# Causal attention with a two-pass softmax on one core: the causal cut of the second pass moves from TensorE to GpSimd

## The reference

```python
scores = jnp.einsum('bhqd,bhkd->bhqk', Q, K) * scale
causal = jnp.triu(jnp.ones((s, s), dtype=bool), k=1)
scores = jnp.where(causal[None, None], -jnp.inf, scores)
attn = jax.nn.softmax(scores, axis=-1)
out = jnp.einsum('bhqk,bhkd->bhqd', attn, V)
```

## Time and profile before

| | |
|---|---|
| median of three runs | 1615.28 us (1613.65 to 1616.12) |
| profiled execution | 1615.37 us, span of its instructions 1613.6 us |
| TensorE (PE) busy | 1501.3 us, 93% |
| VectorE (DVE) busy | 811.3 us, 50% |
| ScalarE (ACT) busy | 545.0 us, 34% |
| GpSimd (POOL) busy | 216.3 us, 13%, nearly all behind 1015 us |
| mean granted TensorE clock | 0.958 of full speed |

### The profile page before, as it was taken

How to read it: one execution, slowest core, us unless ns; L and a number is a source line. 1 busy time by engine, 2 the same in 40 slices (tenths; PEclk the granted TensorE clock), 3 DMA queues, 4 the chain that set the end, 5 groups by cost and what they waited for, 6 DMA issues and landing times.

```text
span 1613.6 us, 22531 instructions
## 1 busy us (share of the span) xinstructions
PE 1501.3 (93%) x6818; PEld 788.3 (49%) x6819; DVE 811.3 (50%) x2073; ACT 545.0 (34%) x1130; POOL 216.3 (13%) x296
## 2 busy tenths in 40 slices
PE   3997999999999997899999966799999999999996
PEld 2553233343433332455555535566666666666663
DVE  2898988888788840666666649211111111111111
ACT  3563176666667676211211110111111111111111
POOL 0000000000000000000000000233333333333332
PEclk9997599999999999899999986899999999999998
DMA  6676400310410000344444320133333333333332
GB/s 200 202 213 199 89 8 5 76 38 5 91 28 5 5 5 15 102 160 146 147 150 145 126 84 0 46 65 65 65 65 65 65 65 65 65 65 65 65 65 33
DMA packets 86078, 127.79 MB, mean 79 GB/s; under 512 B 15822, under 2 KB 48846, under 8 KB 85878
## 3 DMA queue, kind: packets, MB, share of 16 engines
q1 hardware_dynamic: 68038, 87.67, 18.0%
q0 software_dynamic: 16064, 37.76, 13.5%
q10 hardware_dynamic: 1904, 1.46, 0.3%
HBM read 78.17 MB, written 48.50 MB: 78 GB/s over the span
## 4 chain that ended last, share of the span: by engine, by line
PE 85%; DVE 8%; ACT 2%; issue 2%; DMA 2%; ACTq 0%; DVEq 0%; POOL 0%; POOLq 0%; SPq 0%
PE psum L943 31%; PE psum L954 16%; PE psum L853 9%; PE psum L835 8%; PE psum L815 8%; PE psum L769 3%; PE psum L914 3%; PE psum L926 2%; DVE arena L1106 2%; PE psum L903 2%; DVE x L1282 1%; DMA arena<-in_gate 1%; PE psum L838 1%; PE psum L818 1%; ACT arena L607 1%
## 5 line engine op out<-in xcount | busy, mean ns | idle before, releaser
L943 PE MATMUL psum<-arena,xg_t 128*128 (+2 forms) x1648 | 510.2, 463 | 0.2 <-issue 0.2
L943 PEld LDWEIGHTS psum<-arena,xg_t 128*128 128x128 f32 x1648 | 307.0, 191 | 156.7 <-issue 3.7
L1106 DVE TENSOR_REDUCE arena<-psum 128x1 f32<-128x512 f32 (+3 forms) x640 | 348.8, 604 | 65.5 <-PE psum L815 38.7
L677 ACT ACTIVATE arena<-psum 128x512 f32<-128x512 f32 (+3 forms) x640 | 301.5, 535 | 186.3 <-PE psum L838 101.7
L954 PE MATMUL psum<-arena,act_t 128*128 (+3 forms) x618 | 282.5, 593 | 1.3 <-ACT act_t L706 1.3
L1174 DVE TENSOR_TENSOR act_sb<-psum,silu 128x352 f32<-128x352 f32 x103 | 54.1, 525 | 413.0 <-ACT silu L726 413.0
L815 PE MATMUL psum<-arena 96*128 96x512 bf16 (+3 forms) x640 | 230.0, 375 | 11.5 <-DVE arena L1106 10.6
L835 PE MATMUL psum<-arena 99*128 99x512 bf16 (+3 forms) x640 | 214.2, 352 | 3.7 <-ACT arena L677 3.7
L726 ACT ACTIVATE silu<-psum 128x352 f32<-128x352 f32 x103 | 47.8, 464 | 429.9 <-PE psum L943 429.9
L550 POOL COPY cur_i<-idx_i 128x1 int32 (+1 forms) x71 | 52.2, 735 | 1019.0 <-DVE idx_i L1290 1011.8
L954 PEld LDWEIGHTS psum<-arena,act_t 128*128 128x128 f32 (+1 forms) x618 | 117.5, 190 | 121.7 <-issue 99.5
(11 more groups left out here) (137 smaller groups left out, 1010.8 us busy)
## 6 DMA issues: line engine op xcount, KB each, us to landing
arena<-qk_parts SPq DMA_DIRECT2D x48, 256.0 KB, 7.4
arena<-in_w SPq DMA_DIRECT2D x16, 704.0 KB, 4.6
arena<-in_x SPq DMA_DIRECT2D x32, 256.0 KB, 4.3
x<-in_x SPq DMA_DIRECT2D x32, 256.0 KB, 2.9
xn_rows<-xg SPq DMA_DIRECT2D x32, 256.0 KB, 2.1
out_rows<-y_sb SPq DMA_DIRECT2D x32, 256.0 KB, 2.0
qk_parts<-arena SPq DMA_DIRECT2D x16, 384.0 KB, 3.3
v_rows<-arena SPq DMA_DIRECT2D x8, 512.0 KB, 6.0
```

The source lines that it names most:

```text
L677: nc.scalar.activation(probs[:, at_b % PS, d * P:], psum[:, NA + at_b % NBK, 0:CH - d * P], ACT.Exp, scale=float(HD) ** -0.5).then_inc(s_e, 1)
L943: i = nc.tensor.matmul(psum[:, bank + k % 2, 0:w], xg_t[:, k % 2, c, :], rhs, start=c == 0, stop=c == DC - 1)
L1106: nc.vector.tensor_reduce(m_raw[:, n % 2, u, i, j:j + 1], psum[:, at_a % NA, 0:w], AX.X, ALU.max).then_inc(s_ar, 1)
```

## The change

In pass B the mask instruction of line 838 is gone: 256 fewer matrix instructions and as many weight loads. ScalarE takes the exponent of all scores of a diagonal tile. Then GpSimd, for each diagonal group, sets the triangle of the four heads' corners to zero in `probs` with one `affine_select` of 128 x 4 x 128 float32 elements: it waits for the group's fourth exponent (`s_e`) and tells TensorE by a new semaphore (`s_keep`), for which the diagonal group's PV waits. Pass A keeps its mask. A constant "keep" of 128 columns is added to the table that is loaded at the start; nothing reads it.

```diff
@@ constants
-               ("token", TOP_K * NT), ("spare_row", 1)):
+               ("token", TOP_K * NT), ("spare_row", 1), ("keep", P)):
...
+    put("keep", np.where(np.arange(P)[:, None] > np.arange(P)[None], 0, 3e38))
@@ GpSimd's program, behind its two DMAs of zero rows
+            pool.wait_ge(s_c, 16)
+            at_pv = 0
+            for item in plan:
+                if item[0] == "PV":
+                    _, n, un, c, kt = item
+                    d = kt - c * CT
+                    if d >= 0:
+
+                        pool.wait_ge(s_e, (at_pv + 1) * G)
+                        at = at_pv * G % PS
+                        corner = probs[:, at:at + G, d * P:(d + 1) * P]
+                        nc.gpsimd.affine_select(corner, corner, [[0, G], [1, P]], ALU.is_ge, 0.0, base=0, channel_multiplier=-1).then_inc(s_keep, 1)
+                    at_pv += 1
+
             pool.wait_ge(s_idx, 1)
@@ TensorE's program, item B
-                    diagonal = kt >= c * CT
                     ins = nc.tensor.matmul(psum[:, bank, 0:CH - d * P], stack_k[g][0:KM, j, kt * P:(kt + 1) * P],
-                                           stack_q[g][0:KM, j, c * CH + d * P:(c + 1) * CH], start=True, stop=not diagonal)
-                    if diagonal:
-                        ins = nc.tensor.matmul(psum[:, bank, 0:P], identb, cbf("mask_t"), start=False, stop=True)
+                                           stack_q[g][0:KM, j, c * CH + d * P:(c + 1) * CH], start=True, stop=True)
                     ins.then_inc(s_b, 1)
@@ TensorE's program, item PV
                     pe.wait_ge(s_e, (at_pv + 1) * G)
+                    if kt >= c * CT:
+                        pe.wait_ge(s_keep, CT * n + kt - c * CT + 1)
                     for j in range(G):
```

More of the change, by code:

```diff
@@ L333, in program @@
         s_pv = sem("pv_groups_done")
+        s_keep = sem("diagonals_cut")
         s_oe = sem("chunk_output_copied")
```

## The result

The changed kernel takes 1647.47 us (median of four runs, 1646.58 to 1648.19) against 1614.95 for the kernel before: ratio 1.0202, 95% interval 1.0189 to 1.0214. That is 32.5 us slower; the forecast was 1647 us, by a sum of +31.3. The kernel is slower beyond any doubt, but whether by more than 2% the interval leaves open. The profiled execution took 1647.68 us, with a span of 1646.0.

The account below looks back on a forecast made before the run. The prediction took TensorE's queue as the bound, with a loop of PV, product, two exponents, PV. Waits for GpSimd +34.3, masks -3.2 and constant table +0.2 made +31.3 us on 1615.37: forecast 1647 us, range 1626 to 1700.

Parts of the forecast that it names:

- room: In a diagonal group, time from the fourth exponent's end to the PV's first weight load; 64 add up to 22.2 us.
- X: Time from the fourth exponent's end to the PV's start with GpSimd between: two hand-overs of 0.06 and select 0.75, 0.87 us.
- room term: What X exceeds the old room by, paid in all 64 diagonal groups of pass B: +34.3 us.
- the branching loop: Rival, 2 in 100: GpSimd's select branches for each element and takes over 5 us; +317 us, time 1929.
- The masks: Of pass B's 256 removed masks only the third product's, ahead of the third exponent, counts: 64 x 0.05, -3.2 us.
- GpSimd's other work: GpSimd's queue is empty from 4.03 to 1015.83 us and the last select is done before 645 us: cost 0.
- The constant table's +0.2: The constant table loaded at the start grows from 608 KB by 64 KB: +0.2 us.
- The clock: Rival, 7 in 100: TensorE waits more in the diagonals and its granted clock falls, mostly the last 53 us; +22, 1669.
- wrong in kind: Signs against the forecast: lower clock between 195 and 640 us, shorter groups between diagonals, or a gap before the first select.
- The stall is not given back: Forecast counts no give-back; the rival, 6 in 100, has the stall replace waits for banks and masks save 14.3: 1601 us.
- The signs: Expected in the trace: selects of 0.6 to 1.0 us, rooms 0.8 to 0.95, nothing changed in length outside 195 to 680 us.

Follow-up runs that it names:

- experiments 3: The changed kernel with a MEMSET of 128 x 512 float32 into an unused tile ahead of each select: 1688.23 us, ratio to the kernel before 1.0458.
- 4: The changed kernel with four selects of 128 x 128 in each diagonal group, each behind its own head's exponent: 1628.4 us, ratio to the kernel before 1.0083.
- experiment 1: The changed kernel with the mask product on TensorE put back beside GpSimd's select: 1649.6 us, ratio to the kernel before 1.0214.
- experiment 2: The kernel before with pass B's mask product taken out and nothing in its place: 1607.15 us, ratio 0.9952.
- 7: The changed kernel with four selects by head and every PV behind item 3 of the next group instead of item 1: 1608.66 us, ratio to before 0.9964.
- 5: The changed kernel with every PV behind item 3 of the next group instead of item 1: 1608.96 us, ratio to the kernel before 0.9968.
- experiment 6: The kernel before, mask on TensorE and no select, with every PV behind item 3 of the next group instead of item 1: 1614.60 us, ratio 1.0000.
- 8: The changed kernel with only the diagonal groups' PV behind item 3 of the next group instead of item 1: 1609.44 us, ratio to the kernel before 0.9967.

## Why the prediction was right, and where it was off

- **What bounds the kernel** was read rightly: TensorE's queue, with the loop PV, product, two exponents, PV. The room of the earlier trace rows as the only cover is shown by experiments 3 and 4: with it made longer and shorter, the sum of rooms and the time moved with it. The 64 rooms before, each raised to the measured 0.82 where it was less, give +31.3 us; measured are +31.5.
- **X** was 0.82 us, not 0.87. The parts are 0.07 in, 0.636 select and 0.11 out, against 0.06, 0.75 and 0.06. So the room term was +31.5 us instead of +34.3. The select takes 0.12 us more than the MEMSET of the earlier trace rows and 0.06 more than my 0.577 for a copy built from those rows; the addition for its compare was too large. The 769 ns that the Trainium skill's GPSIMD Engine Reference, section 3.1, gives for a tight loop without data-dependent branching over 512 elements would have been too long as well. A select of over 5 us, the branching loop, didn't appear.
- **The masks** were put at -3.2 us beside the select; the trace gives -3.1 ahead of the third exponent, and -1.0 more in the two exponents, which the sum left out (0.9 in experiment 1, 1.2 in experiment 2). I said that up to 14.3 us would be there if the select were free. Experiment 2 shows 7.1: this bound was twice too large, since much of what masks hold lies in time in which TensorE waits for ScalarE anyway.
- **GpSimd's other work at no cost:** right, the sequencer's instruction is at 4.1 us. The last select ended at 668.1 us, not before 645, which was written without the 31 us of the change itself; it cost nothing, since the gathers start behind 1015 us. The constant table's +0.2 can't be seen; the part ahead of the first PV was even 1.5 us shorter in the profiled execution, for which I have no cause.
- **The clock** was a rival with 7 in 100 and its price outside the sum. It was neither the sum nor the rival as I drew it: it fell for 10 and 7 us in the last 40 us of pass B, and for 3.4 us at 465, not throughout. I had named a lower clock between 195 and 640 us as a sign of being wrong in kind, and this sign came. (I also wrote that from 150 to 190 us TensorE waited for VectorE at each product; the profile shows it for 62 of 73.) A PV at the lower level in the changed kernel, and the next at the full one again:

```profile
635.50 1.94 PE L868 MATMUL psum<-arena 128*32 128x512 f32 x8 [0.35 <-ACT arena L704]
...
639.94 1.06 PE L868 MATMUL psum<-arena 128*32 128x512 f32 x8 [0.24 <-ACT arena L693]
```

  With 5.3 us, 4.7 of them at the three drops, it is the term that the sum left out. The first of the two PVs holds TensorE for 1.87 us, where I had written 2.00. So that 1647 met 1647.5 to half a us is luck: the room term was 2.8 us too large, the clock term of 5.3 us was missing, and smaller pieces of either sign (exponents, plain rooms, the parts ahead and behind) come to about -1.4. What was no luck is the mechanism and the size of its main term.
- **The stall is not given back:** right. The plain groups at the full clock kept their times to 0.1 us in 90 of 94 cases.
- **The signs.** The select's length, the rooms (0.82 to 0.86 in the mean of each diagonal) and the parts outside pass B came as named. GpSimd as the releaser was to appear near 60 times with 30 to 60 us and appears 45 times with 28.1, though all 64 PVs wait at least 0.82 us.

That the waits cause the drops of the clock is not shown. In one execution of each kernel, the time at the 1.2 GHz level within pass B is none in the kernel before and in experiments 2 and 7, 3.4 us in 5, 6 and 8, 6.9 in 1, 12.4 in 4, 20.5 in the changed kernel and 63.4 with the MEMSET. In the kernels without the mask and with the early PV (2, 4, the changed one, 3) it grows with the rooms; this speaks for it. But experiment 1 has the rooms of the changed kernel and a third of its time at the lower level, and experiment 6 has one drop with no select at all:

```profile
355.00:359.00 4.00, 3.42 (x18) 1.06 (x17) 2.55 (x7) 0.89 (x2) 0.00 (x0) 0.57 0.15 36
```

So the rooms alone don't decide it, and what does stays open.

## What to carry to other kernels

When work moves to an idle engine, its length counts only against the room that the consumer has: measure, for each place, the time from the last producer's end to the consumer's start, and sum what the new hand-over exceeds. Here an idle engine in a loop of three was dearer than a short instruction on the busy one, until the consumer stood later in its queue: two lines of the plan turned +32 us into -5. A bound from "so many instructions less in the busy queue" was twice too high even on the engine that holds the chain. And a difference of two times can be a net: look at the granted clock of both before reading it as the price of the edit.

## What the runs showed of the hardware

An affine_select of 128 x 512 float32 takes 0.636 us and one of 128 x 128 0.294, so 0.89 ns an element above some 0.18 us. From ScalarE to GpSimd the hand-over was 0.07 us and from GpSimd to TensorE 0.11, where ScalarE to TensorE was 0.05; so most of the 0.81 us in the earlier trace rows, from a COPY to the DMA that waits for it, was something else than such a hand-over. A MEMSET and a select start 0.48 us apart, 0.05 less than the MEMSET's length. TensorE's clock fell to the 1.2 GHz level in the midst of work: in the changed kernel behind diagonal groups with waits of about 1 us each, but once also in experiment 6, which has no select. A PV of 1.00 us then held 1.87.
